# One reciprocal for two heads' softmax sums in the last attention of a decoder kernel

## The reference

```
    x = x + _L1_xattn_ref(_layernorm(x, axis=-1), ctx_1024, ctx_1024, ...)
    x = x + _L1_ffn_ref(_layernorm(x, axis=-1), L1_ffn_weight, L1_ffn_bias)
...
        scores = jnp.einsum('bhqd,bhkd->bhqk', Q, K) / np.sqrt(dk)
        attn = jax.nn.softmax(scores, axis=-1)
        out = jnp.einsum('bhqk,bhkd->bhqd', attn, V)
```

## Time and profile before

| | |
|---|---|
| median of 3 runs | 3489.75 us (3487.76 to 3494.26) |
| span of the profiled execution, first to last instruction | 3485.0 us |
| what lies between that span and the median | 4.75 us |
| mean granted clock of TensorE | 0.947 of full speed |
| share of the span busy: PE, DVE, ACT, POOL | 89%, 60%, 40%, 38% |
| the last phase | from about 2890 us to the end |

### The profile page before, as it was taken

How to read it: one execution, slowest core, us unless ns; L and a number is a source line. 1 busy time by engine, 2 the same in 40 slices (tenths; PEclk the granted TensorE clock), 3 DMA queues, 4 the chain that set the end, 5 groups by cost and what they waited for, 6 DMA issues and landing times. The chain is left out here.

```text
span 3485.0 us, 72178 instructions
## 1 busy us (share of the span) xinstructions
PE 3090.1 (89%) x23752; PEld 2316.5 (66%) x23768; DVE 2080.6 (60%) x5225; ACT 1398.2 (40%) x4587; POOL 1326.2 (38%) x1995
## 2 busy tenths in 40 slices
PE   6999999999997999999758777777689996999997
PEld 5888888888885787787534333333367775676774
DVE  6676666666665878878652111111166676888885
ACT  4444444444443555555431111111021115777774
POOL 2454554554542444444310000000022224888786
PEclk8999999999997999999969989888899998999998
DMA  3001001001002121121269999999821113222221
GB/s 130 19 18 36 18 18 36 18 18 36 18 13 98 37 72 49 48 67 53 77 264 386 426 426 426 424 426 426 336 96 66 66 56 110 72 86 81 71 80 34
DMA packets 151017, 456.07 MB, mean 131 GB/s; under 512 B 13316, under 2 KB 65672, under 8 KB 130472
## 3 DMA queue, kind: packets, MB, share of 16 engines
q1 hardware_dynamic: 129960, 434.27, 32.3%
q10 hardware_dynamic: 20992, 20.98, 1.7%
HBM read 399.63 MB, written 55.57 MB: 131 GB/s over the span
## 5 line engine op out<-in xcount | busy, mean ns | idle before, releaser
L436 POOL TENSOR_TENSOR cross_prob<-cross_prob,cross_rsum 128x128 f32<-128x128 f32 (+1 forms) x512 | 255.9, 531 | 347.0 <-DVE cross_rsum L823 346.8
L436 POOL TENSOR_TENSOR self_prob<-self_prob,self_rsum 128x128 f32<-128x128 f32 (+1 forms) x512 | 285.7, 585 | 246.1 <-DVE self_rsum L823 246.0
L1820 POOL TENSOR_TENSOR last_prob<-last_prob,last_rsum 128x256 f32<-128x256 f32 x512 | 304.6, 627 | 110.3 <-DVE last_rsum L2156 108.2
L677 ACT ACTIVATE self_prob<-self_S,self_neg_max 128x128 f32<-128x128 f32 (+1 forms) x512 | 212.0, 425 | 200.7 <-DVE self_neg_max L815 200.6
L430 POOL TENSOR_TENSOR self_QK_T<-self_QK_T,self_turned 128x512 f32<-128x512 f32 x128 | 164.5, 1285 | 295.0 <-DVE self_QK_T L778 293.2
L1254 PE MATMUL experts_H<-moe_w,experts_tok 128*32 128x512 f32 x1024 | 165.0, 803 | 117.3 <-DMA moe_b<-in_L_ffn_w 106.1
L1477 POOL MEMSET norm_minus_half<- 128x2 f32 x1 | 0.1, 100 | 691.1 <-POOLq L53 691.1
L2035 ACT ACTIVATE last_prob<-last_S,last_neg_max 128x256 f32<-128x256 f32 x512 | 238.1, 491 | 41.5 <-DVE last_neg_max L2152 41.5
L677 ACT ACTIVATE cross_prob<-cross_S,cross_neg_max 128x128 f32<-128x128 f32 (+1 forms) x512 | 210.2, 429 | 76.0 <-DVE cross_neg_max L815 74.9
L1371 DVE COPY experts_hidT<-experts_T 128x512 f32<-128x512 f32 x32 | 22.1, 692 | 323.6 <-PE experts_T L1265 323.6
L1254 PEld LDWEIGHTS experts_H<-moe_w,experts_tok 128*32 128x32 f32 x1024 | 40.8, 141 | 220.7 <-issue 165.3
(11 more groups left out here) (314 smaller groups left out, 9816.4 us busy)
## 6 DMA issues: line engine op xcount, KB each, us to landing
moe_w<-in_L_ffn_w SPq DMA_DIRECT2D x64, 4096.0 KB, 36.3
front_x_t<-in_x SPq DMA_DIRECT2D x16, 512.0 KB, 3.6
self_res<-in_x SPq DMA_DIRECT2D x16, 512.0 KB, 3.6
x<-self_res SPq DMA_DIRECT2D x16, 512.0 KB, 2.8
front_x_t<-x SPq DMA_DIRECT2D x16, 512.0 KB, 5.4
front_spare<-in_ctx SPq DMA_DIRECT2D x16, 512.0 KB, 6.2
cross_res<-x SPq DMA_DIRECT2D x16, 512.0 KB, 3.6
x<-cross_res SPq DMA_DIRECT2D x16, 512.0 KB, 2.8
```

What stands on the lines that cost most here:

```text
L436: ins = pool.tensor_tensor(pr, pr, rsum[:, h, t:t + 1].to_broadcast([P, KQ[t]]), ALU.mult)
L677: ins = act.activation(prob[:, h % NP, SOFF[t]:SOFF[t] + KQ[t]], SC[h % G][:, SOFF[t]:SOFF[t] + KQ[t]], ACT.Exp, bias=neg_max[:, h, t:t + ...
L1820: ins = pool.tensor_tensor(pr, pr, rsum[:, h, t:t + 1].to_broadcast([P, S]), ALU.mult)
```

## The change

`sums_inverse` inverts the sums of head h and of the head before it in one instruction of 128 x 4 values, waits for the exponentials of head h, and raises the semaphore by 2. It is called for the odd heads only. In DVE's order inv0, inv2, ... inv14 are gone, and the odd ones stand elsewhere than before: inv3 behind max5, inv5 behind apply, inv7 behind max9, inv9 behind max11, inv11 behind max13, inv13 and inv15 at their old places, and inv1, for the next batch, at the end behind G0 and G1.

```diff
         "DVE": (
-                "max3 take14- inv1 inv2 z2- stats+ max4 max5 take0 z3- max6 max7 apply+ inv3 inv4 O0- take2 X0+ inv5 max8 max9 "
-                "inv6 X1+ max10 inv7 max11 inv8 inv9 O1- take4 fstats- inv10 max12 take6 max13 fapply- max14 take8 z0 inv11 "
-                "max15 inv12 inv13 inv14 take10 max0+ max1+ max2+ take12 z1 inv15 inv0+ G0- G1-"),
+                "max3 take14- z2- stats+ max4 max5 inv3 take0 z3- max6 max7 apply+ inv5 O0- take2 X0+ max8 max9 "
+                "inv7 X1+ max10 max11 inv9 O1- take4 fstats- max12 take6 max13 inv11 fapply- max14 take8 z0 "
+                "max15 inv13 take10 max0+ max1+ max2+ take12 z1 inv15 G0- G1- inv1+"),
...
             def sums_inverse(n, h):
+
                 dve.wait_ge(exp_ok, n * H + h + 1)
-                dve.reciprocal(rsum[:, h, :], sums[:, h, :]).then_inc(rsum_ok, 1)
+                dve.reciprocal(rsum[:, h - 1:h + 1, :], sums[:, h - 1:h + 1, :]).then_inc(rsum_ok, 2)
```

## The result

The changed kernel takes 3524.55 us in the median of 4 runs (3523.76 to 3527.58), the kernel before on the same chip 3488.76 (4 runs, one more than in the table above, 3487.18 to 3494.26). The ratio is 1.0101, 95% interval 1.0088 to 1.0113: 1% slower, where 3523 us was forecast. The profiled execution spans 3522.9 us, 37.9 more than before.

The account below looks back on a forecast made before the run. The prediction took TensorE (PE), busy 89% of the span, to set the pace. It added 28.4 us of lateness (25.2 + 2.15 + 1.0) and 5 for the clock to 3489.75, giving 3523 us, range 3510 to 3540.

Parts of the forecast that it names:

- The pair 14, 15: Last pair: norm14, fbias and norm15 queue behind inv15, making T15 1.80 us late per boundary, 2.15 at the last.
- Only this pair: Even heads waiting for odd heads: the seven other pairs have cover; without it each would cost nothing to 1.2 us.
- inv11 ahead of fapply: DVE between max13 and the quantising F0 waits for: the moved reciprocal adds 16 x 0.065 = 1.0 us to the path.
- DVE's saved time is worth nothing: On DVE: 128 fewer reciprocals save 8.3 us of its time, or nothing, but nothing on the path, since DVE waits for PE.
- The clock: TensorE's granted clock: new idle at T15 may cause falls of 1.38 us each; bounds 0 and 20.7 us, taken as 5.
- The sum: Whole kernel: 25.2 + 2.15 + 1.0 = 28.4 us of lateness, plus 5 us for the clock.
- The 4.75 us: Whole kernel: median of runs 3489.75 us lies 4.75 above the profiled span of 3485.0, a difference carried into the forecast.
- The first: Rival at T15: same lateness and the clock falls nearly each time, 49.1 us slower, 3539 us; chance 0.12.
- the third: Rival on DVE: not slower, T15 has cover and DVE's saved 8.3 us come back, 3481 us; chance 0.03.
- The second: Rival on the clock: T15 late, but the 6 old falls vanish and none come, 20.1 us slower, 3510 us; chance 0.10.

Follow-up runs that it names:

- e1: The changed kernel with POOL's bias addition fbias put before norm14, not between norm14 and norm15: 3491.54 us, ratio to the kernel before 1.0002.
- e3: The changed kernel with only the pair 14, 15 undone, seven pairs still merged: 3491.55 us, ratio to the kernel before 1.0004.
- e6: The kernel before with one extra reciprocal into an unread spare tile ahead of fapply, inv11 left behind z0: 3487.93 us, ratio 0.9994.
- e2: The changed kernel with only the pair 10, 11 undone, inv10 behind fstats and inv11 behind z0: 3518.66 us, ratio to the kernel before 1.0076.
- e4: The changed kernel with the pairs 10, 11 and 14, 15 both undone, six pairs still merged: 3488.76 us, ratio to the kernel before 0.9996.
- v_merged: v_quiet_pool with the pairs 4, 5 and 12, 13 merged in place, nothing else moved: 3457.1 us, ratio to the kernel before 0.9898.
- e5: The kernel before with inv11, still single, moved from behind z0 to ahead of fapply: 3493.5 us, ratio 1.0010.
- v_quiet_pool: The kernel before, reciprocals single, inv5 to inv11 earlier, norm10 and norm11 ahead of the residual, which waits until both casts are done: 3457.36 us, ratio 0.9907.
- v_no_wait: v_quiet_pool without its added wait, so the residual follows norm11 at once: 3491.67 us, ratio to the kernel before 1.0005.

## Why the prediction was right, and where its sizes were off

- **The pair 14, 15.** Right, and shown from both sides: e1 moves fbias out, e3 takes the merge away, and either one returns T15 to its place. Forecast 1.80 us a boundary, measured 5.18 - 3.28 = 1.90. POOL's hand to PE took about 0.1 more than the 0.06 taken from a DVE row. At the last boundary 2.15 was forecast, and T15 came 2.14 late.
- **Only this pair.** Right in the effect on T: with the other seven merged, PE doesn't wait for POOL in the full periods (e3).
- **inv11 ahead of fapply.** The step was there, but mis-sized and its mechanism wrong: 0.065 us was put down for the instruction, and it costs nothing (e6). I followed what was late behind inv11 on DVE and not whom it sets free: norm11 ran some 2 us earlier, which I noted as harmless, and landed on DVE's casts. It costs 0.41 us a batch in the changed kernel, 14 x 0.41 = 5.7, where 1.0 was forecast for the whole; e2 took it back in each period (35.07 against 35.49).
- **DVE's saved time is worth nothing.** Right: e4, v_merged. The row that the size was bounded by holds too: the reciprocal of two heads takes 0.17 us against 0.15, and the next instruction starts 0.09 behind it against 0.07.
- **The clock.** 5 us were put down for new falls at T15. In 14 full boundaries there was none there; two more than before came behind F0 and T9 in the full periods (2 x 1.37 = 2.7), one less in the 14th, and one at the last T15 after 2.93 us of idle. In that tail the output projection ran at the lower level for about 5 us, as the two windows below show (changed kernel, then the kernel before). From T15 to the last F0 it took 18.5 us where it was 15.8, so this cost some 2.5 us. Together that is 2.7 - 1.4 + 2.5 = 3.8, near the estimate of 5, but by luck: the mechanism put down for it did not occur.

```profile
3495.00:3500.50 5.50, 4.46 (x11) 3.54 (x12) 0.48 (x1) 0.46 (x1) 0.00 (x0) 0.50 0.25 95
```

```profile
3460.00:3465.00 5.00, 4.37 (x19) 3.63 (x20) 1.18 (x2) 0.06 (x1) 0.00 (x0) 1.00 0.05 20
```

- **The sum.** Forecast 28.4 + 5 = 33.4 us; the medians differ by 35.8, the spans by 37.9. The spans' difference is made of 13 full periods, 32.9 (13 x 2.33 = 30.3 and 2.7 of falls), 0.9 in the 14th period (the same 2.3, less the one fall that it had before), 4.9 behind it (2.1 at T15, about 2.5 by the clock), and -0.7 ahead of the first. By cause, that is 14 x 2.33 + 2.1 = 34.7 us of lateness, where 28.4 was forecast, and 3.8 of clock, where 5 was. Of the 6.3 us too little, 4.7 are inv11's (5.7 against 1.0) and 1.4 the 0.10 us a boundary by which T15 came later than forecast. The 4.75 us that the prediction puts between span and median are 2.0 within one execution (3524.9 us for a span of 3522.9); the rest is that the profiled one was faster than most, which is why spans and medians differ by unlike amounts here.
- **Rivals.** The first (a fall at each T15) and the third (DVE decides) are refuted by the windows and by e4. The second, that the clock gives back, did not happen here, but its mechanism is real: e1, e3 and e5 have periods that are worth 8.7, 5.7 and 5.7 us over 14 batches, had fewer falls, and measure only 2.1, 2.1 and 3.5 us more in the median.

What stays open is which batches see a fall: with the same two idles before F0 and T9 (1.17 and 0.50) there were 6, 5 and 9 falls in 13 periods of the kernel before, of e2 and of e4, in one profiled execution of each. No run here tells what decides it, beyond that without the first idle there are none (v_quiet_pool, v_merged).

## What to carry to other kernels

When a wait is merged with a later one, look at what is written behind it on the waiting engine: the head itself had slack, the unrelated bias addition between the two norms had not. When a signal comes earlier, follow whom it wakes and what runs beside the woken work; an engine that starts too soon can cost time as well as one that starts too late (here 0.41 us a batch against 1.90). And where DVE works for a waiting PE, look whether POOL is at work at the same time: holding POOL back for 2.4 us a batch made a kernel that was 0.93% faster than the one before, and without that wait nothing of it was left.

## What the runs showed of the hardware that was not expected

GpSimd's elementwise work and some of DVE's lengthen each other. The quantising of 128x512 f32 to fp8 takes 0.54 us with POOL still (v_quiet_pool), 1.32 and 0.83 in the kernel before with POOL's additions and norm beside it, 1.35 and 1.49 in v_no_wait. The loss isn't shared evenly: POOL's additions stayed at 2.5 to 2.7 us for two, while a row of two norms beside the quantising took 1.56 in place of 1.19.

The Trainium skill ("SBUF — State Buffer", the entry on the shared port pair under Terms) says that DVE and GpSimd share one pair of SBUF ports by an exclusive lock held for a whole instruction, and that the loser blocks fully. The trace agrees as far as it goes: in v_no_wait a DVE instruction of 0.54 us lasts as long as POOL's of 1.3 us beside it. Not every DVE instruction takes part: the row maxima at 3115.65 of the changed kernel take 0.68 us beside norm11, and 0.68 with POOL still at 3072.69 before the change.

A single idle of PE of about 1.5 us before T15 was never followed by a lower granted clock, in 14 cases of the changed kernel and 14 of e2, and one of 0.50 never in the 13 full periods of v_quiet_pool and of v_merged. Idles of 1.15 to 1.73 and 0.50 us around eight short bf16 transposes were, in 4 to 9 of 13 periods over nine kernels. The 2.93 us before the last T15 was followed by a fall both times, in the changed kernel and in e2.
